# Graph weight and key sums finished inside the query stage; the mix stage begins with graph products

## The reference

```python
xn = layernorm(x)
W = zeros((1024, 1024)).at[src, dst].add(edge_weight)      # 41250 edges
x = x + xn @ W.T + gnn_bias + mix(xn)
# mix: q, k, v = split(xn @ W_qkv); q, k = relu(rmsnorm(q) * qn_w), relu(rmsnorm(k) * kn_w)
#      per head (16 of 64): kv = k.T @ v; k_sum = k.sum(0)
#      out = (q @ kv) / (q @ k_sum + 1e-6);  mix = concat(out) @ W_out + b_out
t = rmsnorm(layernorm(x)) * norm_scale
x = x + layernorm(x) + moe(t)   # 8 experts, top 2 of a gate; swiglu, 512 hidden, 256 out of it
```

## Time and profile before

| what | us |
|---|---|
| median of 3 runs | 1178.75 |
| lowest, highest | 1176.22, 1180.52 |
| the profiled execution | 1176.67 |
| its span | 1174.9 |
| PE busy | 956.7 (81%) |
| DVE busy | 785.2 (67%) |
| ACT busy | 271.7 (23%) |
| POOL busy | 166.1 (14%) |

### The profile page before, as it was taken

One profiled execution on the slowest core, in us unless ns is written; L12 is line 12 of the kernel. 1 busy time (PEld: TensorE's weight loads), 2 busy tenths in 40 slices (PEclk: granted clock), 3 DMA queues, 4 the chain that ended last, 5 costly groups with the idle time before them and its releaser, 6 DMA issues.

```text
span 1174.9 us, 18153 instructions
## 1 busy us (share of the span) xinstructions
PE 956.7 (81%) x5569; PEld 594.8 (51%) x5570; DVE 785.2 (67%) x1245; ACT 271.7 (23%) x455; POOL 166.1 (14%) x186
## 2 busy tenths in 40 slices
PE   3428999999999789973698999999728999999940
PEld 2324666666666446541366666566514555555510
DVE  4888788888888698447576666763463555555555
ACT  0652222222222344460011111110002222122100
POOL 1232000000000100000223322221102111111432
PEclk9657999999999989995699989998858999999985
DMA  7545333333333445558913333335318999762759
GB/s 229 177 137 193 123 142 143 143 143 143 142 143 139 179 162 180 187 209 235 299 61 138 122 106 106 106 106 204 127 33 293 309 349 343 274 241 110 210 168 304
DMA packets 86474, 210.27 MB, mean 179 GB/s; under 512 B 29395, under 2 KB 38553, under 8 KB 81321
## 3 DMA queue, kind: packets, MB, share of 16 engines
q1 hardware_dynamic: 70345, 171.27, 42.4%
q0 software_dynamic: 12208, 24.42, 6.9%
q10 hardware_dynamic: 3888, 14.16, 3.0%
HBM read 128.37 MB, written 81.42 MB: 179 GB/s over the span
## 4 chain that ended last, share of the span: by engine, by line
PE 44%; DVE 20%; issue 15%; DMA 8%; SPq 4%; ACT 4%; POOL 2%; DVEq 1%; POOLq 0%; ACTq 0%
PE windows L882 11%; PE bank L721 9%; PE bank L900 6%; PE bank L777 6%; PE bank L822 4%; DMA arena<-in_w_flat 3%; DMA arena<-y_dram,arena 2%; DVE arena L1347 2%; DVE arena L1254 2%; PE bank L873 2%; POOL arena L611 1%; SPq L443 1%; PE windows L740 1%; DVE arena L1247 1%; DVE arena L1260 1%
## 5 line engine op out<-in xcount | busy, mean ns | idle before, releaser
L822 PE MATMUL bank<-arena 128*125 128x512 f16 x960 | 220.7, 389 | 2.7 <-POOL arena L594 2.7
L721 PE MATMUL bank<-arena 128*125 128x512 f16 x960 | 217.5, 384 | 0.0
L822 PEld LDWEIGHTS bank<-arena 128*125 (+1 forms) x960 | 133.8, 140 | 78.5 <-issue 7.2
L721 PEld LDWEIGHTS bank<-arena 128*125 (+1 forms) x960 | 129.6, 138 | 73.2 <-issue 3.8
L882 PE MATMUL windows<-arena 128*128 x648 | 149.7, 381 | 0.0
L777 PE MATMUL bank<-arena 128*128 128x416 f16 (+1 forms) x576 | 103.7, 340 | 0.0
L882 PEld LDWEIGHTS windows<-arena 128*128 128x128 f16 x648 | 63.8, 98 | 65.7 <-issue 1.6
L1254 DVE SCALAR_TENSOR_TENSOR arena<-arena 128x2048 f16<-128x2048 f32 x32 | 73.0, 2285 | 12.7 <-ACT arena L972 12.7
L777 PEld LDWEIGHTS bank<-arena 128*128 128x128 f16 x576 | 55.7, 97 | 44.5 <-issue 0.6
L900 PE MATMUL bank<-arena 128*128 x324 | 74.3, 379 | 1.7 <-DVE arena L1527 1.7
L1247 DVE TENSOR_TENSOR arena<-windows,arena 128x1024 f32 x49 | 59.8, 1220 | 16.1 <-issue 8.2
(11 more groups left out here) (223 smaller groups left out, 1285.6 us busy)
## 6 DMA issues: line engine op xcount, KB each, us to landing
arena<-in_w_flat SPq DMA_DIRECT2D x32, 1024.0 KB, 6.5
split_dram<-arena SPq DMA_DIRECT2D x64, 512.0 KB, 3.8
arena<-split_dram SPq DMA_DIRECT2D x48, 512.0 KB
y_dram<-arena SPq DMA_DIRECT2D x9, 1536.0 KB, 6.5
y_dram<-arena ACTq DMA_DIRECT2D x27, 512.0 KB
arena<-in_x SPq DMA_DIRECT2D x20, 448.0 KB
arena<-in_w_qkv SPq DMA_DIRECT2D x8, 1024.0 KB, 6.2
arena<-split_dram SPq DMA_DIRECT2D x32, 256.0 KB, 6.3
```

The lines of the kernel that those rows point to most:

```text
L721: mm = pe.matmul(bank[b][0:TT, :], xt[:, l, k, tok(i)], wkv[:, r, k, c0:c0 + 512], start=(k == 0 and n == 0), stop=(k == KT - 1 and n == 2))
L822: mm = pe.matmul(bank[half][0:TT, :], a_[:, l, k, tok(i)], w_[:, r, k, c0:c0 + 512], start=(m == 0 and k == 0 and c == 0), stop=(m == 1 an ...
```

## The change

Five things are moved or rewritten; the amount of matmul work stays the same.

1. `make` writes its key matrix into one of the result buffers, and makes the high product in place behind the low one, with one more wait. DVE no longer makes groups 49 and 50, which nobody used.
2. The two conversions of pieces 22 and 23 on DVE move behind the first units of the query stage; `kv_split` (the low parts of the key sums, with fewer and wider operations) moves into the first turn, and ACT's and DVE's splits of the graph weight into the second turn.
3. SP issues the first query weights before the key stage is over, writes the graph weight to `wg_dram` after turn 1's query weights, reads it back after turn 2's, and loads `wo` by high and low part instead of by column half.
4. Mix begins with the graph products (`xt`, `wg`) of tiles 0 and 1, with attention units between them, and an accumulation always starts with the graph product. Tile 0 accumulates in `windows`.
5. Attention units 6 and 7 of a group move from the odd tile of the pair before to the even tile that needs them; POOL, ACT and DVE follow.

```diff
 def make(n, s):   # DVE
-    v.tensor_tensor(pairs_of(key_hot), columns, cols(key16), ALU.is_equal).then_inc(hot_key, 1)
-    v.wait_ge(hot_key, n + 1)
-    v.tensor_tensor(pairs_of(one_hot[s][:, 1, :]), pairs_of(key_hot), cols(whi), ALU.mult)
-    v.tensor_tensor(pairs_of(one_hot[s][:, 2, :]), pairs_of(key_hot), cols(wlo), ALU.mult).then_inc(hot_ready, 1)
+    key_hot = pairs_of(one_hot[s][:, 1, :])
+    v.tensor_tensor(key_hot, columns, cols(key16), ALU.is_equal).then_inc(hot_key, 1)
+    v.wait_ge(hot_key, 2 * n + 1)
+    v.tensor_tensor(pairs_of(one_hot[s][:, 2, :]), key_hot, cols(wlo), ALU.mult).then_inc(hot_key, 1)
+    v.wait_ge(hot_key, 2 * n + 2)
+    v.tensor_tensor(key_hot, key_hot, cols(whi), ALU.mult).then_inc(hot_ready, 1)
...
 # SP, query stage
+load_wq(0, 0)
 sp.wait_ge(kv_mm, 4 * NT)
-for h in range(2):
-    load_wq(0, h)
+load_wq(0, 1)
+next_pieces(-1)
+for t in range(2):
+    next_pieces(t)
+    next_wq(t)
 for k in range(KT):
     sp.wait_ge(acc_lo, k + 1)
...
+next_pieces(2)
+next_wq(2)
 sp.wait_ge(acc_out, 16 * 2 * KT)
...
+next_pieces(3)
...
+load_wo(0)
...
+sp.wait_ge(eps_mm, 3)
+load_wo(1)
...
 # POOL, mix
+for j in range(2):
+    attend_lo(j, 1, PAIRS + j)
...
-with pool.Fori(0, NT // 2 - 1) as t:
-    for h in range(2):
-        for j in range(4 * h, 4 * h + 4):
-            attend_lo(j, t + 1, PAIRS * (t + 1) + j)
-        mix_out(2 * t + h, h)
-        mix_in(2 * t + h + 2, h, t + 1)
+for j in range(2, 3):
+    attend_lo(j, 1, PAIRS + j)
+mix_out(0, 0)
+mix_in(2, 0, 1)
+for j in range(3, 6):
+    attend_lo(j, 1, PAIRS + j)
+mix_out(1, 1)
+mix_in(3, 1, 1)
+with pool.Fori(1, NT // 2 - 1) as t:
+    attend_lo(6, t, PAIRS * t + 6)
+    attend_lo(7, t, PAIRS * t + 7)
...
 # PE, a tile of mix
 def mix_tile(i, h, t, attend=True):
+    for half in range(2):
+        pe.wait_ge(x1_half, 2 * i - 1 + half)
+        if h == 0:
+            attend_unit(6 + half, t, PAIRS * t + 6 + half)
+        elif attend:
+            attend_unit(2 + half, t + 1, PAIRS * (t + 1) + 2 + half)
+        mix_part(i, bank[0:2], 0, half, 0, KT)
     if h == 0:
         pe.wait_ge(at_done, START + PAIRS * (t + 1))
     for half in range(2):
...
+        if attend:
+            j = 4 * h + half
+            attend_unit(j, t + 1, PAIRS * (t + 1) + j)
+        mix_part(i, bank[0:2], 1, half, 0, KT)
...
 # DVE, query stage (kv_split behind unit 2 of turn 0, acc_part_lo behind units 3 to 5 of turn 1)
+q_turn(0, 6, first=True)
+q_turn(1, Q_GROUPS - 6, split=True)
+q_turn(2)
+q_turn(3, last=True)
```

More of the change, by code:

```diff
@@ L799, in attend_unit, with mix_part @@
                 mm.then_inc(at_mm, 1)
+            def mix_part(i, o, m, half, a, b):
+                a_, w_ = ((xt, wg), (ut, wo))[m]
+                c0 = half * 512
+                for k in range(a, b):
+                    for c, (l, r) in enumerate(((0, 0), (0, 1), (1, 0))):
+                        mm = pe.matmul(o[half][0:TT, :], a_[:, l, k, tok(i)], w_[:, r, k, c0:c0 + 512],
+                                       start=(m == 0 and k == 0 and c == 0), stop=(m == 1 and k == KT - 1 and c == 2))
+                if m == 1 and b == KT:
+                    mm.then_inc(mix_mm, 1)
@@ L800, in _ @@
+            pe.wait_ge(acc_done, START + GROUPS)
+            pe.wait_ge(wg_in[0], 32)
+            mix_part(0, bank[6:8], 0, 0, 0, 4)
+            pe.wait_ge(q_split, START + 6 * KT)
+            pe.wait_ge(q_evac, START + 3 * KT)
+            for g in range(3):
+                pe.matmul(bank[g][:, 0:GRP[g][1]], ones, qss[:, g, 0:GRP[g][1]], start=True, stop=True).then_inc(eps_mm, 1)
+            mix_part(0, bank[6:8], 0, 0, 4, 8)
             pe.wait_ge(eps_ready, 3)
+            pe.wait_ge(wg_in[1], 32)
@@ L801, in _ @@
+            ahead = [(0, 1, 0), (0, 1, 4), (1, 0, 0), (1, 0, 4), (1, 1, 0), (1, 1, 4)]
             for j in range(PAIRS):
                 attend_unit(j, 0, j)
-            def mix_tile(i, h, t, attend=True):
+                if j < len(ahead):
+                    i, half, k = ahead[j]
+                    mix_part(i, (bank[6:8], bank[0:2])[i], 0, half, k, k + 4)
+            for hl in range(2):
+                pe.wait_ge(wo_in[hl], 16 * N_PIECE_O)
+            pe.wait_ge(at_done, START + PAIRS)
```

238 lines of the change are left out of this document (127 added, 111 removed).

## The result

The changed kernel took 1234.49 us (median of 4 runs, 1232.69 to 1239.01) against 1179.63 for the kernel before in the same comparison: 1.047 times the time, interval 1.043 to 1.051. The forecast was 1235, slower. The profiled execution took 1235.16 us, its span is 1233.4.

The account below looks back on a forecast made before the run. It took mix to be paced by POOL's queue and SP's store-and-load round trip, not PE. Key stage +2.7, query +41, transition -28 and mix +42 on 1176.67 gave 1234.4, taken as 1235 us; range 1209 to 1255.

Parts of the forecast that it names:

- What bounds the kernel: Mix loop of before: looks PE-bound, but runs at the pace of POOL's queue and SP's store-and-load round trip, 27.05 us a tile.
- Key stage, +2.7: Key stage: make's extra wait costs 0.22 us, PE waits at one group in four; 0.27 x 10 tiles, +2.7 us.
- Query start, +11: Start of query stage: piece 22 converted later, so piece 24 lands late; PE waits 21 us instead of 9.9, +11.
- Third turn, +16: Query stage, third turn: stores and asks for pieces stand behind SP's 16 graph writes, PE stands still; +16 us.
- Last turn, +11: Query stage, last turn: the 4 MB graph read goes ahead of asks for pieces 30 and 31; 8.2 plus 2.6, +11 us.
- Clock, +3: Query stage: PE runs at the low clock after three more long waits; +3 us.
- Transition, -28: From end of query to mix_out(1): PE starts graph products at once, splits and the wait for wo gone; -28 us.
- Mix loop, +42: Mix loop: attend_lo 6 and 7 stand behind the odd tile's mix_in; 66.4 us a pair against 54.1, +42 us.
- A: Rival: pieces of the query stage's last two turns not delayed, query +11 instead of +41; 1205 us, chance 0.12.
- B: Rival: mix loop keeps 27 us a tile, x sooner or attend_lo not held; 1192 us, chance 0.08.
- C: Rival: PE decides, not the queues, if odd tile's mix_in ends within 13 us of its last matmul; 1130 to 1165, chance 0.07.

Follow-up runs that it names:

- e3: Kernel before with only POOL's order changed: mix_in behind the next tile's four attend_lo; 1158.50 us, ratio 0.983.
- e1: Kernel before with only the change's new make, which has one more wait on DVE; 1182.65 us, ratio 1.004.
- e5: Changed kernel with DVE's conversions of pieces 22 and 23 put back ahead of the query stage's first addition; 1226.11 us, ratio 1.042.
- e13: Changed kernel with the 16 graph writes issued from POOL's queue instead of SP's; 1221.33 us, ratio 1.037.
- e7: Changed kernel with the 16 graph writes in rows of 2 KB instead of 256 B, same volume and queue place; 1229.13 us, ratio 1.044.
- e12: e9 with all eight attention units of a group in the two tiles before it is read, on all four engines; 1135.82 us, ratio 0.964.
- e10: Kernel before with POOL's order of e3, and make's low-digit comparison moved behind the key comparison; 1150.79 us, ratio 0.978.
- e2: Changed kernel with POOL's mix_in moved behind the next tile's attend_lo; 1190.93 us, ratio 1.010.
- e4: Changed kernel with SP's stores and asks for pieces moved ahead of the graph writes and the graph read; 1215.65 us, ratio 1.031.
- e9: e6 plus the make order of e10 and the last turn's first query weights between the 8th and 9th graph write; 1152.52 us, ratio 0.978.
- e6: Changed kernel with three orders repaired together: those of e2 (POOL), e4 (SP) and e5 (DVE); 1166.20 us, ratio 0.990.

## Why the prediction was right, step by step

**What bounds the kernel.** Right, and shown by e3: the mix loop of before had 20 us in it that PE's busy share hid.

**Key stage, +2.7.** Too small; +5.0 measured, +4.7 by e1. The price of a wait (0.22) was right, the count was not: I took one make a tile on the path, and there are two.

**Query start, +11.** Right, and 4 too high in the sum. The waits forecast were 5, 10.9 and 5; they are 3.7, 9.3 and 3.8. The chain (piece 22 converted late, so piece 24 asked for late) is confirmed by e5, which takes the first link away.

**Third turn, +16.** Right in its place, mixed in its make-up. The wait is 13.9. Piece 28 was to land 29 us after the first graph write was issued; it landed by 515.6, 26.5 behind it. The size of the step was wrong in one input: I used the 215 GB/s of the earlier trace rows; here the writes ran at 259. Why the same writes were slower in before isn't known; they ran at 197 to 233 GB/s nearly through that whole stretch. At the full rate the term was to be 7 instead of 16; with large rows e7 measured 8.8. What I called the wait for landing is, by e13, mostly SP's time at the writes, and 8.4 of those 16.7 us are DVE's time for the low parts that the writes wait for. The sum has no term for that, so that it came out near is luck in part.

**Last turn, +11.** 9.2. Piece 30 landed 21.9 us after the graph read was first issued, forecast 21.7. The 2.6 for piece 31 were not seen on PE.

**Clock, +3.** Mis-sized. The query stage lost 39.0 us, of which the waits are 39.8 - 9.9 = 29.9. The other 9 are slower matmuls: the same work kept PE busy 9.2 us longer, at a mean granted clock of 0.87 instead of 0.96. The stage as a stretch (length, busy us and count by engine, clock, DMA share, GB/s), of before and of after:

```profile
395.70:522.70 127.00, 117.06 (x762) 68.11 (x762) 79.42 (x103) 59.81 (x99) 1.58 (x4) 0.96 0.56 203
```
```profile
400.70:566.70 166.00, 126.22 (x763) 71.68 (x764) 93.64 (x131) 61.72 (x93) 1.58 (x4) 0.87 0.61 206
```

That I came out at +41 for a measured +39 is luck in part: waits 8 too many, clock 6 too few.

**Transition, -28.** -27.1. PE goes from query straight into the first graph product (566.52), as forecast. The inner steps held as well: PE passes its wait for group 0 34.4 us behind the end of query (forecast 34.6), mix_out(0) starts at 56.6 (55.3), mix_out(1) at 81.3 (80). e12 shows that nothing behind the transition eats the gain once the order is mended (mix takes 191.8 as in e10).

**Mix loop, +42.** +42.1; pairs of 65.4 to 67.1 (forecast 66.4), waits of 12.6 to 15.6 us for attend_lo at four even tiles (forecast 10 to 14), and 24 matmuls in 6.2 to 7.7 us behind three of them. e2 shows the cause. It gave back 43.6.

**Rivals.** A (pieces not delayed, 1205) and B (the loop keeps 27 us a tile, 1192) didn't come true by themselves, but e4 and e2 are these two cases made by hand: 1215.65 and 1190.93. A was priced 10 too low, since the query weights take the place of the pieces behind the writes. C, the other side (1130 to 1165), failed exactly at its stated point, mix_in of the odd tile; e9 and e12, where POOL's order no longer decides, lie in its range. That range was too wide for its own terms, though: 51 us less, and 2.7 to 13.7 more, make 1128 to 1139. e12 (1135.82) is in that, e9 (1152.52) isn't.

Two sums are off by little: mix_in(0) in the transition is 42 + 5.25 = 47.3 and not 47.9, and with the 2.1 us from profiled execution to median the forecast would be 1236.5 and not 1235.

What stays open: how the 8.8 us left in e7 divide between the wait for DVE's low parts, SP's issue and the load on the DMA engines, since e13 changed packets and issuer at once; and 2 us that e3 gained behind the end of mix, which I didn't trace. The start of the key sums differs by some 1 to 2.5 us between kernels with the same code up to there (400.7 and 401.9; 395.5 and 398.0), so terms of that size are read from medians only.

## What to carry to other kernels

An instruction that waits long for a transfer belongs behind everything in its queue that someone else is waiting for; look at what stands behind each waiting row, not at the wait itself, which may cost its own engine nothing. A loop in which PE is busy 95% can still be paced by a queue: add up the closed chain of the other engines for one round, and if it comes to the period, PE is not the bound. When work is moved into an earlier stage, count what it does to the order of every queue it goes through; here three such places cost about 70 us. Compare with a kernel before that has had the same care, too: against before as it was, the repaired change (e6) gains 1%, against before with POOL's order repaired it loses 7.7 us, and only e12 is ahead, by 15.

## What the hardware showed that I had not expected

In the key stage a DVE step that waits for the step right in front of it starts 0.83 us after that one's start, 0.60 without the wait, and 0.60 with the wait if one independent step stands between (128 x 1024 f16, e10). In the query stage of before the same waiting step starts after 0.72 us (422.02 to 422.74); why it is less there isn't known. The same 4 MB of strided writes went as packets of 256 B from SP's queue and as 1280 packets of 3.3 KB from GpSimd's (e13). SP stood at 16 transfers of 256 KB for 16.7 us with rows of 256 B and for 11.0 us with rows of 2 KB, 8.4 us of each until DVE's last low part; it stood there for 23.0 us when four stores and two asks had been issued just ahead (e4). In the earlier trace rows, where it took 18.0 us, the low parts end 7.9 us behind the first write, at 536.6.
